# Attention weights packed without zeros in a graph network's second part, and 64 by 64 quarter matmuls with half of x copied across partitions by DMA

## The reference, cut to what matters

```python
si = x @ attn_w[l, :d]
sj = x @ attn_w[l, d:]
scores = si[:, :, None] + sj[:, None, :] + attn_b[l]
scores = jnp.where(scores >= 0, scores, 0.2 * scores)
scores = jnp.where(mask, scores, -jnp.inf)
attn = jax.nn.softmax(scores, axis=-1)
agg = jnp.einsum('bij,bjd->bid', attn, x)
h = layernorm(x + agg, g1[l], beta1[l])
ff = jax.nn.gelu(h @ W1[l] + b1[l], approximate=False) @ W2[l] + b2[l]
x = layernorm(h + ff, g2[l], beta2[l])
```

## Time and profile before

| | |
|---|---|
| median of 3 runs | 1718.87 us (1718.17 to 1725.38) |
| profiled execution | 1720.1 us, its span 1718.3 us |
| PE busy | 1613.6 us, 94% of the span |
| PEld busy | 1428.4 us, 83% |
| DVE busy | 1430.9 us, 83% |
| ACT busy | 1164.4 us, 68% |
| POOL busy | 912.5 us, 53% |
| mean granted TensorE clock | 0.978 of full speed |

### The profile page before, as it was taken

The page is one execution under the profiler, slowest core; times in us unless marked ns, Lnnn a source line. Parts: engine busy times, 40 slices in busy tenths (PEclk is TensorE's granted clock), DMA queues, the critical chain, the costliest instruction groups (busy, mean ns, idle before and its releaser), DMA issues. The chain is left out here.

```text
span 1718.3 us, 34331 instructions
## 1 busy us (share of the span) xinstructions
PE 1613.6 (94%) x10304; PEld 1428.4 (83%) x10304; DVE 1430.9 (83%) x4369; ACT 1164.4 (68%) x2059; POOL 912.5 (53%) x1008
## 2 busy tenths in 40 slices
PE   5899999982999999999999999999999999999995
PEld 5678878872889889888898988889889888888895
DVE  3889999986888888988888888888888988888862
ACT  1677777761667776676776776767767677677673
POOL 1567777762345445464554555635445455454464
PEclk9999999995999999999999999999999999999998
DMA  6222222214000001110000011100001110000001
GB/s 175 65 93 92 79 79 83 85 50 147 1 1 1 1 17 31 41 50 27 1 1 3 30 46 36 50 3 1 2 16 31 53 38 26 1 1 1 1 26 49
DMA packets 52968, 65.97 MB, mean 38 GB/s; under 512 B 25681, under 2 KB 42321, under 8 KB 52817
## 3 DMA queue, kind: packets, MB, share of 16 engines
q1 hardware_dynamic: 51184, 57.84, 10.5%
q0 software_dynamic: 816, 3.15, 0.6%
q10 hardware_dynamic: 816, 3.15, 0.5%
HBM read 38.95 MB, written 25.17 MB: 37 GB/s over the span
## 5 line engine op out<-in xcount | busy, mean ns | idle before, releaser
L761 ACT ACTIVATE bank<-bank,b_col 128x512 f32<-128x512 f32 x384 | 252.9, 659 | 349.7 <-PE bank L709 346.4
L721 PE MATMUL bank<-w_hi,hid_hi 128*128 128x256 f32 x1536 | 440.2, 287 | 11.2 <-DVE hid_lo L924 7.2
L721 PE MATMUL bank<-w_hi,hid_lo 128*128 128x256 f32 x1536 | 433.2, 282 | 0.0
L721 PE MATMUL bank<-w_lo,hid_hi 128*128 128x256 f32 x1536 | 432.6, 282 | 0.0
L924 DVE TENSOR_TENSOR hid_lo<-bank,hid_hi 128x512 fp32r<-128x512 f32 x384 | 259.5, 685 | 153.9 <-ACT hid_hi L766 152.6
L709 PE MATMUL bank<-nT_hi,w_hi 128*128 128x512 f32 x768 | 321.2, 418 | 6.6 <-issue 5.2
L721 PEld LDWEIGHTS bank<-w_hi,hid_hi 128*128 128x128 f32 x1536 | 289.3, 188 | 39.2 <-DVE hid_lo L924 27.0
L709 PE MATMUL bank<-nT_hi,w_lo 128*128 128x512 f32 x768 | 304.1, 396 | 0.0
L709 PE MATMUL bank<-nT_lo,w_hi 128*128 128x512 f32 x768 | 303.2, 395 | 0.0
L721 PEld LDWEIGHTS bank<-w_lo,hid_hi 128*128 128x128 f32 x1536 | 289.4, 188 | 11.5
L721 PEld LDWEIGHTS bank<-w_hi,hid_lo 128*128 128x128 f32 x1536 | 289.2, 188 | 0.0
(11 more groups left out here) (122 smaller groups left out, 3363.1 us busy)
## 6 DMA issues: line engine op xcount, KB each, us to landing
xin<-in_x_dram SPq DMA_DIRECT2D x16, 512.0 KB, 3.9
first_block_out<-x_res SPq DMA_DIRECT2D x16, 512.0 KB, 2.7
second_block_in<-x_act SPq DMA_DIRECT2D x16, 512.0 KB, 3.5
x_cur<-second_block_in SPq DMA_DIRECT2D x16, 512.0 KB, 3.9
x_fin<-first_block_out SPq DMA_DIRECT2D x16, 512.0 KB, 3.7
out_dram<-x_fin SPq DMA_DIRECT2D x16, 512.0 KB, 2.9
raw_weights<-in_L_gnn_W_dram ACTq DMA_DIRECT2D x3, 1024.0 KB, 8.4
raw_weights<-in_L_gnn_W_dram POOLq DMA_DIRECT2D x3, 1024.0 KB, 6.4
```

Of the source, the lines that this page charges most:

```text
L721: mm = pe.matmul(FF[t // 2][:, (t % 2) * D:(t % 2 + 1) * D], a[:, r, t * P:(t + 1) * P], w[:, l, c, :], start=(c == 0 and t % 2 == 0 and p ...
L761: act.activation(h[:], h[:], ACT.Gelu, bias=b1_col[:, l, c:c + 1]).then_inc(s_gelu, 1)
```

## The change

Weights of tile t and tile t + 2 (of one group) now stand side by side in one 128 by 128 square, with no zeros. One transpose turns both; the weights of tile t come out on partitions 0 to 63 and those of tile t + 2 on 64 to 127, each with both graphs side by side in the columns. The aggregate is then, for each of two squares, four matmuls of 64 rows by 64 columns of weights (both tiles, both graphs) with 256 columns of x. Two of the four need x on the other half of the partitions; SP copies those halves into `x_other` with two DMAs of 128 KB for each slot, two slots ahead. PE waits for them with a `pause`.

```diff
-            attn = sb("attn", [P, TG, P], where=second)
-            attn_T = sb("attn_T", [P, TG, P], where=second)
+            TP = TG // 2
+            attn = sb("attn", [P, TP, 2, N], where=second)
+            attn_T = sb("attn_T", [P, TP, P], where=second)
+            x_other = sb("x_other", [P, 2, TP, D], where=second)
...
+                def exchange(i, s):
+
+                    l, g = layer_group(s)
+                    V = i * SLOTS + s
+                    pause(sp, s_agg, V - 1, s_own_sp)
+                    if l == 0:
+                        pause(sp, s_in[g], 32 * (i + s // SLOTS + 1), s_own_sp)
+                    else:
+                        pause(sp, s_x, 4 * (V - QG) + 12, s_own_sp)
+                    pause(sp, s_xo, 32 * V, s_own_sp)
+                    sp.dma_start(x_other[0:N, s % 2], x_cur[N:P, g, 0:TP]).then_inc(s_xo, 16)
+                    sp.dma_start(x_other[N:P, s % 2], x_cur[0:N, g, TP:TG]).then_inc(s_xo, 16)
+
+                def some(i, which, last):
+                    for s in which:
+                        nxt, nxt2, nxt3 = ahead(s, last)
+                        g = s - (L - 1) * QG
+                        if nxt2:
+                            exchange(i, s + 2)
+                        if 0 <= g - 2:
+                            put_out(i, g - 2, not last)
+                        if 0 <= g + 1 < QG and not last:
+                            refill(i, g + 1)
...
+                def all_before():
+                    before()
+                    exchange(0, 0)
+                    exchange(0, 1)
...
                 def turn_attn(V, s):
-                    pe.wait_ge(s_at, GPT * (V + 1))
-                    for t in range(TG):
-                        mm = pe.transpose(ATT_T[:, t * P:(t + 1) * P], attn[:, t, :], ident[:])
+                    pe.wait_ge(s_at, V + 1)
+                    for t in range(TP):
+                        mm = pe.transpose(ATT_T[:, t * P:(t + 1) * P], attn[:, t].rearrange("p e j -> p (e j)"), ident[:])
...
                 def aggregate(V, s):
-                    l, g = layer_group(s)
-                    pe.wait_ge(s_atk, V + 1)
-                    for t in range(TG):
-                        mm = pe.matmul(AGG[t // 2][:, (t % 2) * D:(t % 2 + 1) * D], attn_T[:, t, :], x_cur[:, g, t, :],
-                                       start=True, stop=True)
+                    l, q = layer_group(s)
+                    pause(pe, s_atk, V + 1, s_own_pe)
+                    pause(pe, s_xo, 32 * V + 32, s_own_pe)
+                    for t in range(TP):
+                        for e in range(2):
+                            for g in range(GPT):
+                                rows = slice(e * N, (e + 1) * N)
+                                value = x_cur[rows, q, e * TP + t, :] if e == g else x_other[rows, s % 2, t, :]
+                                mm = pe.matmul(AGG[e][g * N:(g + 1) * N, t * D:(t + 1) * D],
+                                               attn_T[rows, t, g * N:(g + 1) * N], value, start=True, stop=True)
...
                 def exp(V, s):
-                    for g in range(GPT):
-                        act.activation(attn[g * N:(g + 1) * N, :, g * N:(g + 1) * N],
-                                       shifted2[g * N:(g + 1) * N], ACT.Exp).then_inc(s_at, 1)
+                    act.activation(attn[:].rearrange("p t e j -> p e t j"),
+                                   shifted2[:].rearrange("p (e t) j -> p e t j", e=2), ACT.Exp).then_inc(s_at, 1)
...
-                    act.copy(attn_T[:].rearrange("p t i -> p (t i)"), ATT_T[:]).then_inc(s_atk, 1)
+                    act.copy(attn_T[:].rearrange("p t i -> p (t i)"), ATT_T[:, 0:TP * P]).then_inc(s_atk, 1)
...
-                dve.memset(attn[:], 0.0).then_inc(s_zero, 1)
...
-                    dve.tensor_reduce(row_sum[:], attn[:], AX, ALU.add).then_inc(s_inv, 1)
+                    dve.tensor_reduce(row_sum[:].rearrange("p (e t) -> p e t", e=2), attn[:].rearrange("p t e j -> p e t j"),
+                                      AX, ALU.add).then_inc(s_inv, 1)
```

More of the change, by code:

```diff
@@ L585, in graph_net @@
             s_out = [sem(f"group_stored{i}") for i in range(2)]
-            s_own, s_own_sp, s_zero = sem("vector_paused"), sem("sync_paused"), sem("attn_zeroed")
+            s_own, s_own_sp, s_own_pe, s_xo = sem("vector_paused"), sem("sync_paused"), sem("tensor_paused"), sem("x_other_ready")
             s_hid, s_gelu, s_hi, s_split, s_ff = sem("hidden"), sem("gelu"), sem("hidden_hi"), sem("hidden_split"), sem("ff_chunk")
@@ L639, in before, with refill, put_out @@
                         load_res(0, g)
[L641 to L646, removed]
+                def refill(i, g):
+                    pause(sp, s_u, TG * (i * SLOTS + (L - 1) * QG + g + 1), s_own_sp)
+                    load(i + 1, g)
+                def put_out(i, g, more):
                     n = i * QG + g
@@ L653, in put_out, with after @@
                         load_res(i, g + 2)
-                    elif not last:
+                    elif more:
                         load_res(i + 1, g - 2)
[L657 to L668, removed]
+                def exchange(i, s):
[19 more added lines that the diff above has]
+                            refill(i, g + 1)
+                def after(U):
+                    for g in range(QG - 2, QG):
+                        put_out(LAPS - 1, g, False)
+                def all_before():
+                    before()
+                    exchange(0, 0)
+                    exchange(0, 1)
+                slots(sp, all_before, some, after)
             @blk.tensor
@@ L797, in before @@
                 def before():
-                    act.wait_ge(s_zero, 1)
                     exp(0, 0)
@@ L1008, in scores @@
                     score.wait()
-                    at_least(dve, s_at, GPT * V)
+                    at_least(dve, s_at, V)
                     dve.tensor_tensor(shifted2[:], leaky2[:], top2[:].unsqueeze(2).broadcast_to([P, TG, N]),
@@ L1013, in row_sums @@
                 def row_sums(V):
-                    dve.wait_ge(s_at, GPT * (V + 1))
-                    dve.tensor_reduce(row_sum[:], attn[:], AX, ALU.add).then_inc(s_inv, 1)
+                    dve.wait_ge(s_at, V + 1)
+                    dve.tensor_reduce(row_sum[:].rearrange("p (e t) -> p e t", e=2), attn[:].rearrange("p t e j -> p e t j"),
+                                      AX, ALU.add).then_inc(s_inv, 1)
                 def row_invs(V):
```

## The result

Over its runs the changed kernel takes 1700.72 us in the median (1697.57 to 1703.42, four runs), the kernel before 1722.12 (1718.17 to 1728.19, four runs): a ratio of 0.9875 with a 95% interval of 0.983 to 0.9919. The same kernel timed once more beside the experiments took 1700.52 against 1720.18, 0.9882 [0.9861, 0.9902]. The profiled execution took 1703.42 us, 2.7 above the median (span 1701.6, mean granted clock 0.974).

A forecast was written before the change was run, and what follows sets the result against it. PE bounds the slot from `output(7)` to `turn_n`, POOL and DVE from there to `low(7)`. 33 x 0.62 = 20.5 plus 13 x 0.26 = 3.4, less 2 at the start, is 21.9 off 1720.1: 1698, range 1692 to 1740.

The forecast's parts named there:

- The two chains: From `output(7)` round the slot: DVE to `low(0)`, 0.45 us in hand; POOL through `post` and `make_base`, 0.36 in hand.
- plain slot: Steady slot where `diagonal` makes no mask, 26.23 us long; 33 of them were to gain 0.62 each.
- mask slot: Slot where `diagonal` also makes a layer 0 mask and `low(0)` is late; 13 were to gain 0.26 us each.
- X: PE's whole time for the new aggregate in a slot, taken as 1.2 us; PE's part shrinks by 1.95 - X.
- rival A: Aggregate on PE: strict order makes a product's second pass hold all behind it; 1.94 to 2.1 us, 1718 to 1725, chance 0.2.
- Transposes: PE's transposes go from four to two per slot, saving 0.22 of 0.45 us.
- Row sums: DVE sums 256 instead of 512 columns ahead of `low(0)`: 0.68 to 0.42 us, 0.26 off DVE's chain.
- ACT's copy and `exp`: One `exp` instruction and a 256-column copy on ACT: nothing on the path; copy there at 989.9, aggregate due at 990.22.
- Exchange: SP's two 128 KB DMAs per slot: nothing in steady slots; 2 us charged at the start, bounds 0 to 5.
- B: Aggregate on PE: quarters held by order and also by their own bare loads; 2.6 us, 1749 in all, chance 0.13.
- C: Aggregate on PE: quarters run one after another; 3.8 us at the worst, 1803 in all, chance 0.12.
- D: Aggregate on PE takes between 1.35 and 1.75 us, so plain slots gain less; 1699 to 1710, chance 0.1.

The follow-up runs named there:

- The run with the columns only: Changed kernel with all quarter products reading partitions 0 to 63, so only the array's two column halves are used; 1726.61 us.

## Why the prediction was right

Forecast 1698 in a range of 1692 to 1740, measured 1700.7 and 1700.5. By its own steps:

**The two chains.** The plain slot was put at 0.62 less, 25.6, and is 25.64 against 26.23, 0.59 less. The dots follow `make_base` and `low(7)` follows them, as said. But the prediction gave DVE 0.71 and POOL 0.62 and let POOL be last; it was the other way round, and that the smaller of the two came to the same number is luck. DVE: the 0.45 in hand took 0.05 behind `low(0)` as the least distance that costs nothing. At that distance `output(0)` takes 0.1 more. In the median of the plain slots `output(0)` started 0.49 behind `low(0)` before and starts 0.06 behind it now, so DVE had 0.49 - 0.06 - 0.10 = 0.33, and allows 0.33 + 0.27 = 0.60. That is what was gained. POOL: its wait of 0.24 was counted as 0.20 in hand, though back to back it would start 0.04 before the end of the one before, which makes 0.28. With the 0.16 ahead of `post` and the 0.27 of the row sum it allows 0.71, and 0.1 of it is left, the distance seen ahead of `make_base`. The prediction's own sign that `low(0)` would hold `output(0)` in nearly all slots came true, and it fits DVE's leg, not POOL's.

The mask slot was put at 0.26 less; measured 0.27, by `low(0)` as said. The slots should give 20.5 + 3.4 = 23.9 and gave 23.1; with the start, 21.9 was forecast and 20.9 measured. The two long slots, which the prediction had counted as plain ones, gave 2.2 for 1.2; the other 44 gave 20.9 for 22.6. In the changed kernels here the two are between 28.9 and 30.5 long, so part of the closeness of the sum is luck too.

**The aggregate.** X was taken as 1.2 between 0.86 + 0.35 and 3.44 + 0.35; it is 1.23. Its parts were right as well: four at a time at 0.216, and 0.37 around them where 0.35 was estimated. No row gave the 0.08 that the estimate took for a change of shape; the runs show 0.09 ahead of the quarters and 0.22 behind them, and 0.05 in the longer first round. That X needed no exact value, since any up to 1.33 gives the same slot, is what the two runs with doubled products show: 0.12 of the added PE time vanishes in both. Which part of the 0.09 ahead of the quarters is the `pause` and which the change of shape wasn't tried apart; nor was PE's gap of 0.22 behind them.

The Trainium skill (TensorE: Matmul & The Clock Gate, Part 3: Packing small matmuls) has starts 4 ns apart on different tiles. The trace has 0.02 us over the three steps of a round, so nearly that. It also says that matmuls keep program order in start and end, which carried rival A. The trace doesn't show a second pass that holds the quarters behind it: all four first passes start ahead of the first second pass. Whether the passes stand in this order already in what PE is given, no run here shows.

**Transposes.** Half of 0.45 was to go. The two cost 985.56 - 985.11 = 0.45 less one step of `hidden`, 0.23, so 0.22 are left and 0.23 gone.

**Row sums.** 0.42 forecast, 0.41 measured, and the run with the wide sum shows that all of it counts.

**ACT's copy and `exp`.** The aggregate isn't held by the copy in any steady slot; the first quarter starts 0.54 behind the copy's end in each of them, where 0.14 is enough when the copy does hold it (the first aggregate of the run without exchange). The waits in front of it are those of the sequencer.

**Exchange.** Nothing in steady slots, as the run without it shows. At the start 2 us were charged and 2.2 measured. The first exchange was to land near 414, 19.7 after the first load, and its second copy landed 20.8 after it. The first aggregate started 3.9 later than before, where 3 was taken; it is 1.8 shorter (1.98 against 3.78), where 1 was taken, and 3.9 - 1.8 = 2.1. So two steps were each mis-sized by about 1 and cancel. The sign against it, a first aggregate past 417, was 22.7 after the first load; the trace has 20.9, and its 419.76 is past 417 only because the whole second part began 4.55 later. The earlier trace rows had the DMA engines done soon after 411; in the profile after they stay busy for longer. Against a start without the exchange the cost is more than the 2.2: the run without it gained 2.8 at the first slot's `hidden`, of 5.1 at the aggregate's start.

**Rivals.** A (X 1.94 to 2.1), B (2.6), C (3.8) and D (1.35 to 1.75) are all excluded by X = 1.23. The run with the columns only shows what A would have looked like in time: 1.98 from the first quarter, and 1726.6 us, no gain.

Where single expectations missed, it was by a term left out: 0.10 in the runs with doubled products (the gap ahead of the first quarter), and 0.16 in the version with one tile's dots moved (a third collision with POOL).

## What to carry to other kernels

When two chains are within a few tenths of a microsecond of each other, cost an edit against both: here PE gave up 0.72 per slot, and the time fell by what DVE's chain allowed, 0.6. Adding small known amounts to each chain afterwards tells which one sets the end, and how much the other has in hand, better than busy shares do. It tells this only for the stretch where the amount is added. Where two legs join, look which release keeps the same distance in every slot: `make_base` stayed 0.08 behind `turn_n`, and not behind `post`. And a wait's least distance is the one at which the next step takes no longer, not the least that a row shows. The next gain then lies in the order of the work on the chain that sets the end: moving two of the dot products and the mask brought more (23 us, by 1700.5 and 1677.7) than halving the aggregate's work had (20 us).

## What was unexpected of the hardware

DVE's dot products, which read two buffers, and the instructions of `make_base` on POOL slow each other down. The dot product takes 0.42 alone and up to 1.48 beside `make_base`; the POOL pair it meets goes from 2.55 to 2.72 with one such meeting and 2.91 with two, 0.17 to 0.19 each. So moving a DVE instruction within its own slack isn't free when it moves onto POOL's work. The Trainium skill (SBUF — State Buffer, Who interferes with whom) says that a DVE instruction with two SBUF inputs contends with a GpSimd one that reads SBUF; the runs here agree: without the second half of `make_base` both dots fell to 0.42.

Four quarters of the array, and also two column halves on the same 64 rows, ran side by side here, at 0.216 us for a round of 256 columns at the full clock, with four quarters in a round or with two.

A copy of 128 KB issued behind a full set of loads landed 8.4 us after its issue, where the median of all these copies is 2.4 us (`x_other`, from issue to landing):

```profile
DMA to landing us min/median/max: 2.2/2.4/8.4
```
